# A two-layer graph network on one Trainium2 core: the cross scores turned by VectorE in 32 by 32 blocks

## What is computed

```
u     = h @ h.T / sqrt(384)              # 64 x 64 scores of a graph
a     = softmax(u) ; delta = a * adjacency
attn  = delta / (sum(delta) + 1e-10)
ctx   = (attn above the diagonal) @ (h Wl + bl)
      + diag(attn) * (h Ws + bs)
      + (attn below the diagonal) @ (h Wr + br)
out   = relu(layernorm(ctx) * gamma + beta)
```

## Time and profile before

| | |
|---|---|
| median of three runs | 1221.5 us |
| profiled execution, its own time | 1221.17 us |
| its span in the trace | 1219.4 us |
| granted TensorE clock over the span | 0.995 of full speed |
| PE, PEld, DVE, ACT, POOL busy | 99%, 98%, 87%, 81%, 26% |

### The profile page before, as it was taken

The page is one execution under the profiler, slowest core; times in us unless marked ns, Lnnn a source line. Parts: engine busy times, 40 slices in busy tenths (PEclk is TensorE's granted clock), DMA queues, the critical chain, the costliest instruction groups (busy, mean ns, idle before and its releaser), DMA issues.

```text
span 1219.4 us, 26362 instructions
## 1 busy us (share of the span) xinstructions
PE 1202.2 (99%) x7067; PEld 1197.1 (98%) x7067; DVE 1060.2 (87%) x2863; ACT 982.4 (81%) x2673; POOL 312.1 (26%) x421
## 2 busy tenths in 40 slices
PE   8899999999999999999999999999999999999997
PEld 7899999999999999999999999999999999999997
DVE  6789898989888888888888888998989899998976
ACT  6677777778777788888888888888888888888874
POOL 2223223232222121122212121223333232323221
PEclk9899999999999999999999999999999999999999
DMA  5434343433232323333333323322332323332321
GB/s 181 129 95 126 109 128 98 128 92 117 91 108 72 96 86 117 106 124 116 111 115 105 106 87 104 114 85 96 98 108 97 108 96 96 103 96 98 100 92 55
DMA packets 112960, 127.63 MB, mean 105 GB/s; under 512 B 11104, under 2 KB 100192, under 8 KB 112864
## 3 DMA queue, kind: packets, MB, share of 16 engines
q1 hardware_dynamic: 112864, 126.50, 33.1%
HBM read 76.91 MB, written 49.55 MB: 104 GB/s over the span
## 4 chain that ended last, share of the span: by engine, by line
PE 96%; ACT 1%; DVE 1%; DMA 1%; issue 1%; SPq 0%; POOL 0%; POOLq 0%; DVEq 0%; ACTq 0%
PE left_bank L474 24%; PE context_bank L474 24%; PE right_bank L474 24%; PE context_bank L505 17%; PE score_bank L450 6%; DMA rows<-weights 1%; PE edge_bank L458 0%; ACT weight L696 0%; DMA nodes<-squares 0%; DVE weight L906 0%; ACT nodes L579 0%; PE edge_bank L464 0%; SPq L365 0%; DVE context L963 0%; ACT side_parts L643 0%
## 5 line engine op out<-in xcount | busy, mean ns | idle before, releaser
L474 PE MATMUL left_bank<-weight,node_t 128*128 128x384 f32 x1728 | 337.5, 338 | 0.0
L474 PE MATMUL context_bank<-weight,node_t 128*128 128x384 f32 x1728 | 332.6, 337 | 4.6 <-ACT context_bank L653 4.6
L474 PE MATMUL right_bank<-weight,node_t 128*128 128x384 f32 x1728 | 333.5, 337 | 1.1 <-DVE weight L906 1.1
L474 PEld LDWEIGHTS context_bank<-weight,node_t 128*128 128x128 f32 x1728 | 303.5, 189 | 5.2 <-ACT context_bank L653 4.9
L474 PEld LDWEIGHTS left_bank<-weight,node_t 128*128 128x128 f32 x1728 | 303.6, 188 | 0.0
L474 PEld LDWEIGHTS right_bank<-weight,node_t 128*128 128x128 f32 x1728 | 299.2, 188 | 1.5 <-issue 1.5
L505 PE MATMUL context_bank<-side_parts,attn_t 128*128 128x386 f32 x1152 | 239.4, 343 | 2.1 <-issue 2.1
L505 PEld LDWEIGHTS context_bank<-side_parts,attn_t 128*128 128x128 f32 x1152 | 199.4, 189 | 3.5 <-issue 2.8
L643 ACT ACTIVATE side_parts<-right_bank 128x384 fp32r<-128x384 f32 x192 | 94.3, 491 | 128.4 <-PE context_bank L505 128.4
L1145 POOL TENSOR_TENSOR rstd<-spread,scalars 128x2 f32<-128x2 f32 x95 | 68.3, 719 | 498.1 <-DVE spread L941 498.1
L816 DVE TENSOR_TENSOR node_t<-nodes,node_t 128x768 fp32r<-128x768 f32 x94 | 145.5, 1548 | 9.4 <-ACT node_t L584 9.1
(11 more groups left out here) (88 smaller groups left out, 1593.3 us busy)
## 6 DMA issues: line engine op xcount, KB each, us to landing
squares<-turned SPq DMA_DIRECT2D x94, 384.0 KB, 2.7
nodes<-squares SPq DMA_DIRECT2D x376, 96.0 KB, 2.2
rows<-x SPq DMA_DIRECT2D x64, 384.0 KB, 4.0
out<-rows SPq DMA_DIRECT2D x31, 384.0 KB, 2.6
adj_in<-adj SPq DMA_DIRECT2D x96, 64.0 KB, 1.9
piece<-weights SPq DMA_DIRECT2D x18, 192.0 KB, 2.5
rows<-weights SPq DMA_DIRECT2D x3, 576.0 KB, 8.1
vector_rows<-vectors SPq DMA_DIRECT2D x3, 384.0 KB, 3.8
```

The costliest lines, as they stand in the source:

```text
L474: mm = nc.tensor.matmul(bank[:, 0:D], node_t[:, s.parity, k, c, a], weight[:, s.phase % 2, w, c, b], start=False, stop=(c, a) == (CH - 1, ...
```

## The change

In phases 0 (from its third step) and 2, TensorE no longer turns the cross scores. ScalarE copies them out as before (two copies of 64 x 128), but no longer packs them (the two copies of 64 x 64 go). After `seed_side(s, 1, LEFT)` it makes eight copies of 32 x 64 from SBUF to SBUF, which exchange the blocks of 32 by 32 between quarters of the partitions. VectorE then turns all blocks in one transpose of 128 x 128 into `own_edge` (which is free between `diagonal` and the next `place_edges`), and `add_cross` adds that. VectorE's transpose stands ahead of `norm(prev, 0)` in both phases: in phase 0 it is put straight before it, and `add_cross` still follows behind that `norm`; in phase 2 the order is now the two `gather_input` (moved to the front), the transpose, `add_cross`, `spreads(prev)`, `norm(prev, 0)`. Phase 1, and the first two steps, keep the product.

```diff
+FIRST_BY_BLOCKS = 2
+def by_blocks(s):
+    return s.bounded and not (isinstance(s.n, int) and s.n < FIRST_BY_BLOCKS)
...
+        cross_flat = cross[:, 0].rearrange("p (k j) -> p k j", k=2)
+        cross_moved = cross[:, 1].rearrange("p (k b j) -> p k b j", k=2, b=2)
+        turned_blocks = own_edge[:, :, :].rearrange("p k j -> p (k j)")
...
                 project_side(s, 1, RIGHT)
-                if nxt.exists():
+                if nxt.exists() and not by_blocks(nxt):
                     turn_cross(nxt)
...
             def copy_cross(s):
                 act.wait_ge(scored, s.n + 1)
-                at_least(act, cross_turned, s.n)
                 at_least(act, score_summed, 2 * s.n)
+                if by_blocks(s):
+                    act.wait_ge(cross_added, s.n)
+                    for half in HALVES:
+                        nc.scalar.activation(cross_flat[half], scores4[half, :, 1, half], ACT.Copy).then_inc(cross_packed, 1)
+                    return
...
+            def move_blocks(s):
+                act.wait_ge(cross_packed, packed_before(s) + 2)
+                copied = cross_flat.rearrange("p k (b j) -> p k b j", b=2).bitcast(F32)
+                for q in range(QUARTERS):
+                    r, here, other = q % 2, q * Q, (q ^ 1) * Q
+                    nc.scalar.activation(cross_moved[here:here + Q, :, r], copied[here:here + Q, :, r], ACT.Copy).then_inc(blocks_moved, 1)
+                    nc.scalar.activation(cross_moved[here:here + Q, :, 1 - r], copied[other:other + Q, :, r], ACT.Copy).then_inc(blocks_moved, 1)
...
                 seed_side(s, 1, LEFT)
+                if nxt.exists() and by_blocks(nxt):
+                    move_blocks(nxt)
...
             def sum_scores(s):
-                dve.wait_ge(cross_packed, 4 * (s.n + 1))
+                dve.wait_ge(cross_packed, packed_before(s) + (2 if by_blocks(s) else 4))
...
+            def turn_blocks(s):
+                dve.wait_ge(blocks_moved, 2 * QUARTERS * (block_index(s) + 1))
+                nc.vector.transpose(turned_blocks, cross[:, 1].bitcast(F32)).then_inc(blocks_turned, 1)
...
+                if by_blocks(s):
+                    dve.wait_ge(blocks_turned, block_index(s) + 1)
+                    nc.vector.tensor_tensor(score[:, :, :], score[:, :, :], own_edge[:, :, :], ALU.add).then_inc(cross_added, 1)
+                    return
...
+                if nxt.exists() and by_blocks(nxt) and s.phase < 2:
+                    turn_blocks(nxt)
                 if prev.exists() and not prev.level():
                     norm(prev, 0)
+                if nxt.exists() and by_blocks(nxt) and s.phase == 2:
+                    if fourth.exists():
+                        gather_input(fourth, 0)
+                        gather_input(fourth, 1)
+                    turn_blocks(nxt)
                 if nxt.exists():
                     add_cross(nxt)
...
                 if prev.exists() and prev.level():
                     spreads(prev)
-                if s.phase != 1 and fourth.exists() and fourth.bounded:
+                if s.phase == 0 and fourth.exists() and fourth.bounded:
                     gather_input(fourth, 0)
                     gather_input(fourth, 1)
```

More of the change, by code:

```diff
@@ L96, in slot, with block_index, turn_index, packed_before @@
         return bass.ds(2 * self.g + k, 1)
+FIRST_BY_BLOCKS = 2
+def by_blocks(s):
+    return s.bounded and not (isinstance(s.n, int) and s.n < FIRST_BY_BLOCKS)
+def block_index(s):
+    return s.normal - FIRST_BY_BLOCKS
+def turn_index(s):
+    return s.n if s.phase == 0 else s.n - PAIRS + FIRST_BY_BLOCKS
+def packed_before(s):
+    if s.phase == 0:
+        return 2 * s.n + 2 * (min(s.n, FIRST_BY_BLOCKS) if isinstance(s.n, int) else FIRST_BY_BLOCKS)
+    phase_one = 2 * PAIRS + 2 * FIRST_BY_BLOCKS
+    return phase_one + 4 * s.g if s.phase == 1 else phase_one + 4 * PAIRS + 2 * s.g
 def at_least(eng, sem, value):
@@ L261, in adj_gnn_program @@
         cross_turned = sem("cross_turned")
+        blocks_moved = sem("blocks_moved")
+        blocks_turned = sem("blocks_turned")
         cross_added = sem("cross_added")
@@ L454, in turn_cross @@
             def turn_cross(s):
-                pe.wait_ge(cross_packed, 4 * (s.n + 1))
+                pe.wait_ge(cross_packed, packed_before(s) + 4)
                 at_least(pe, cross_added, s.n)
@@ L593, in copy_cross @@
                 act.wait_ge(scored, s.n + 1)
-                at_least(act, cross_turned, s.n)
                 at_least(act, score_summed, 2 * s.n)
+                if by_blocks(s):
[3 more added lines that the diff above has]
+                    return
+                if s.phase == 1:
+                    act.wait_ge(cross_added, s.n)
+                else:
+                    at_least(act, cross_turned, s.n)
                 for h, half in enumerate(HALVES):
@@ L829, in sum_scores @@
             def sum_scores(s):
-                dve.wait_ge(cross_packed, 4 * (s.n + 1))
+                dve.wait_ge(cross_packed, packed_before(s) + (2 if by_blocks(s) else 4))
                 for h, half in enumerate(HALVES):
-                    nc.vector.tensor_tensor(score[half], scores4[half, :, 0, half], cross_here[h].bitcast(F32),
+                    copied = cross_flat[half] if by_blocks(s) else cross_here[h]
+                    nc.vector.tensor_tensor(score[half], scores4[half, :, 0, half], copied.bitcast(F32),
                                             ALU.add).then_inc(score_summed, 1)
+            def turn_blocks(s):
+                dve.wait_ge(blocks_moved, 2 * QUARTERS * (block_index(s) + 1))
+                nc.vector.transpose(turned_blocks, cross[:, 1].bitcast(F32)).then_inc(blocks_turned, 1)
             def add_cross(s):
-                dve.wait_ge(cross_turned, s.n + 1)
                 dve.wait_ge(score_summed, 2 * s.n + 2)
+                if by_blocks(s):
+                    dve.wait_ge(blocks_turned, block_index(s) + 1)
+                    nc.vector.tensor_tensor(score[:, :, :], score[:, :, :], own_edge[:, :, :], ALU.add).then_inc(cross_added, 1)
+                    return
+                dve.wait_ge(cross_turned, turn_index(s) + 1)
                 nc.vector.tensor_tensor(score[:, :, :], score[:, :, :], turned_cross, ALU.add).then_inc(cross_added, 1)
```

## The result

The changed kernel takes **1296.05 us** (median of four runs, 1295.69 to 1296.26) against 1221.24 for the kernel before on the same chip (four runs): a ratio of **1.0608, interval 1.0596 to 1.062**. That is 74.8 us lost where 46.7 were forecast, and 3 us beyond the top of the range. The profiled execution took 1296.26 us with a span of 1294.4, so its rows speak for the median.

What follows compares the result with a forecast made beforehand. TensorE, never stopping mid-kernel, was taken as the bound. Phase 2's 45.8 us lost, less 2 for written-out steps, plus 2.9 in phase 0, gave 46.7 us on 1221.17: 1268 us, range 1234 to 1293.

Steps and rivals of the forecast that it cites:

- The lateness arrives there whole, less the margin: Phase 2, VectorE's left split: 1.72 us late less margins of 0.20 and 0.38, mean loss 1.43 us a step.
- mean margin of 0.29: Phase 2 loop: the left split reaches TensorE's weighing with 0.20 and 0.38 us to spare in alternate steps.
- the end of the addition: Phase 2, VectorE: the addition behind the transpose ends at 1000.26 in place of 998.54, 1.72 us late.
- Other waits are looser: Phase 2: ScalarE's right split moves from 999.26 to 1000.23, with 0.70 idle before it; VectorE doesn't wait for it.
- the one result that reaches TensorE last: VectorE's left split of tile 1, margin 0.20 or 0.38 us in phase 2, 0.26 or 0.80 in phase 0.
- The 4.2 us: Phase 0: nine steps that split new weights, margin 0.26, each lose 0.47 us at the left split.
- What goes: TensorE loses 62 turning products of 0.06 us, 3.7 us at most; ScalarE loses two copies, 0.48 us a step.
- Free moves: Rival: ScalarE's eight copies overlap, 0.145 apart, and end 0.98 us earlier, giving 1234; chance 0.15.
- VectorE's idle time takes it all: Rival: VectorE's idle 1.36 and 0.99 us in phase 2 steps absorb transpose and wait, giving 1217.8; chance 0.04.
- ScalarE becomes the bound: Rival: ScalarE gains 1.68 us in each of 62 steps, giving 1325.5 with its stops at TensorE kept; chance 0.04.
- a gap of TensorE somewhere else: Sign that the forecast is wrong: TensorE idle elsewhere than in front of the left half of the weighing.
- the top of the range, 1293: Upper bound: one copy taking 0.299 us adds 0.43 or 0.36 us a step, 25 us.

Runs made afterwards that it cites:

- p0_only: The change made in phase 0 alone, phase 2 keeping the TensorE product: 1244.05 us, ratio 1.0173 to the kernel before.
- half_moves: The changed kernel without the four copies that keep a block in its quarter: 1237.31 us, ratio 1.0125 to the kernel before.
- psum_moves: The changed kernel with four 32 x 64 copies from PSUM, after the sums, in place of eight copies: 1240.06 us, ratio 1.0144 to the kernel before.
- no_moves: The changed kernel without all eight copies, the transpose reading the first copied scores: 1222.18 us, ratio 1.0004 to the kernel before.
- early_square: psum_moves with, in phase 2, square ahead of the first copies, spreads ahead of the sums, norm ahead of the transpose: 1216.29 us, ratio 0.9949 to the kernel before.
- seed_first: The changed kernel with ScalarE's square and tile 1's self seed ahead of the eight copies: 1343.11 us, ratio 1.0984 to the kernel before.
- twice_turned: The kernel before with the turning product issued twice in all 96 steps: 1231.93 us, ratio 1.0084 to the kernel before.

## Why the prediction was wrong in size

Of the 28.1 us between forecast and measurement 17.6 lie in phase 0 and 8.4 in phase 2.

**Right in direction and in mechanism for phase 2.** As it said: the moves delay the transpose, VectorE is idle in front of it (1.27 us), the lateness runs through `norm(prev, 0)` to the left split, and TensorE stops before the left half of the weighing. "The lateness arrives there whole, less the margin" held: 1.97 less the mean margin of 0.29 is 1.68, 0.07 more was added between the addition and the left split, and the loop's steps grew by 1.77. The loss of 52.2 against 43.8 is a mis-sized term, the end of the addition: 4.97 after the scores, forecast 4.72. The 0.25 fall apart into 0.06 for a later start of the first move (2.02 after the scores in place of 1.96), 0.09 for eight pitches of 0.28 in place of 0.267 (one copy takes 0.255, not 0.245), 0.02 for the transpose (0.31, not 0.29), and 0.08 for a gap of 0.11 between transpose and addition, where 0.03 was put.

**Wrong in phase 0.** The step that failed is the sentence "Other waits are looser: ScalarE's right split moves from 999.26 to 1000.23, with 0.70 idle before it now, and VectorE, late itself, doesn't wait for it." It stands under phase 2; for phase 0 the forecast looked at no wait but the left split's. What it says of the right split is true, but ScalarE's queue goes on behind it: the next instruction is `seed_self(s, 1)`, and for that TensorE does wait, with a margin of 0.23. Had I followed the queue one instruction further, phase 0 would have come out at about 0.7 lost in each of 18 steps, near the measured 0.77: the forecast's moves end at 278.57, the seed ends 1.55 behind the last move (241.79 less 240.24), so 0.94 late, less the margin of 0.23. The forecast looked for "the one result that reaches TensorE last", and took the smallest margin of one step for the only one: the left split's 0.26 in phase 0, while the seed's 0.23 stood beside it and was hit by the larger delay (1.03 against 0.73). The 4.2 us that it put there, nine waits at the left split, did not come: with TensorE held up for the seed, none is longer than 0.15 in its 28 steps. p0_only shows these 20.8 us by themselves, half_moves and psum_moves that they go as soon as ScalarE has a microsecond less to do.

**What goes: half the price.** Removing the product gives 0.127 a step (12.347 to 12.220 in no_moves), not 0.06, about 7.9 us over 62 steps and not "3.7 us at most". It didn't show in the result, since both phases were set by waits; it shows in early_square.

**The rivals.** *Free moves* falls: eight copies run at a pitch of 0.28, each starting 0.02 after the one before ended, those with only another output partition too (238.31 and 238.59). Each of the seven behind the first starts at another partition than the one before, in its input or its output; no run has two such copies in a row that don't, so that this keeps them apart is argued, not shown, and the first, which starts at partition 0 as the seed before it does, comes 0.02 behind the seed's end as well (238.03 and 238.01). *VectorE's idle time takes it all* falls for this order of work, but early_square is nearly that case, made by hand: with `norm(prev, 0)` in front of the transpose the idle time does take the moves. *ScalarE becomes the bound* was set aside for the right split; its true part is phase 0, where ScalarE's queue sets the step without ScalarE being busy throughout it (11.39 of 13.12 us).

**The signs.** L458, now L489, went from 96 to 34, the pitch was 0.28 where 0.27 stood, VectorE's idle time and the stop of TensorE at the left half were there. The sign of error was there too: "a gap of TensorE somewhere else". And the top of the range, 1293, was reached with a slower copy alone; no bound stood for a wait that had been overlooked.

## What to carry to other kernels

When work is put into an engine's queue, follow every instruction behind it on that queue up to the next stop that is long enough to take up the delay, and ask of each who waits for it and with what margin; the first one that is harmless proves nothing for the next. On an engine that is full, take the price of a small instruction from the length of a step with it and without it, or doubled, not from the distance of two starts. Idle times of one step are not a sum to be won: taking the wait of the shorter of two loops away, at the price of later moves, made the step longer (seed_first), and the gain of a removed product came only when its substitute was cut to half and the work that others wait for was put ahead of it.

## What the runs showed that was not expected

- A product of 128 columns among products of 384 costs 0.11 to 0.13 us (twice_turned, no_moves), twice the distance between its start and the next: the products behind it pay the other half, 1.28 in place of 1.21 for six.
- ScalarE's 32 x 64 copy takes 0.255 us from SBUF to SBUF and 0.215 from PSUM to SBUF (psum_moves).
- The transpose of 128 x 128 in blocks of 32 takes 0.31 us, the addition of that size 0.29; the blocks' exchange between the quarters, more than the transpose, is what the change pays for: eight copies 2.2 us, four from PSUM 0.93 (in early_square).
- TensorE's granted clock fell to 0.50 for some 3.4 us in nine steps of seed_first (phase 2), which cost 14 us; a forecast by stops alone doesn't see that.
